# A fused attention and gate kernel: the first group's weights taken from the prepared tiles, the first loads on two DMA queues

## The reference

```
x   : 4 x 512 x 1024          xn = layernorm(x)
q, k, v = xn @ Wq.T, xn @ Wk.T, xn @ Wv.T     # 32 query heads, 8 key/value heads, 128 wide
q, k = rmsnorm(q) * q_norm_w, rmsnorm(k) * k_norm_w
scores = q k^T / sqrt(128) + slope[head] * (pos_k - pos_q), masked above the diagonal
s = softmax(scores) v  @ Wo.T
g = silu(xn @ W.T + bias + sum_n 2 * lora_weights[n] * (xn @ A_n.T) @ B_n.T)
out = x + s * g
```

## Time and profile before

| | before |
|---|---|
| median of 3 runs | 2731.64 us |
| profiled execution | 2726.47 us, span 2724.6 us |
| mean granted clock of TensorE | 0.985 |
| TensorE busy | 2591.6 us, 95% |
| VectorE, ACT, GpSimd busy | 1648.0, 1769.1, 1726.9 us |
| chain that ended last | TensorE 88%, VectorE 3%, ACT 2%, GpSimd 2%, DMA 2% |

### The profile page before, as it was taken

One profiled execution on the slowest core, in us unless ns is written; L12 is line 12 of the kernel. 1 busy time (PEld: TensorE's weight loads), 2 busy tenths in 40 slices (PEclk: granted clock), 3 DMA queues, 4 the chain that ended last, 5 costly groups with the idle time before them and its releaser, 6 DMA issues.

```text
span 2724.6 us, 39884 instructions
## 1 busy us (share of the span) xinstructions
PE 2591.6 (95%) x13840; PEld 2296.2 (84%) x13840; DVE 1648.0 (60%) x3520; ACT 1769.1 (65%) x4627; POOL 1726.9 (63%) x845
## 2 busy tenths in 40 slices
PE   2759999999999999999999999999999999999997
PEld 2648888888888888888888888888888888888886
DVE  4536655656667656566566665557566756555656
ACT  2246666666866766766776676666776667667763
POOL 2467787886667665656576666566565856656553
PEclk8879999999999999999999999999999999999999
DMA  7777778877345333433335433433334433433323
GB/s 234 261 263 262 251 249 274 266 257 247 118 149 166 117 122 111 142 113 103 119 94 175 149 109 115 141 110 111 109 107 142 165 122 99 122 117 109 116 69 128
DMA packets 183095, 424.48 MB, mean 156 GB/s; under 512 B 33520, under 2 KB 74608, under 8 KB 182000
## 3 DMA queue, kind: packets, MB, share of 16 engines
q1 hardware_dynamic: 182896, 421.93, 48.1%
HBM read 349.51 MB, written 89.13 MB: 161 GB/s over the span
## 4 chain that ended last, share of the span: by engine, by line
PE 88%; DVE 3%; ACT 2%; POOL 2%; DMA 2%; issue 1%; SPq 1%; POOLq 0%; DVEq 0%; ACTq 0%
PE proj L488 21%; PE proj L490 21%; PE proj L489 21%; PE tr L581 5%; PE sc L488 3%; PE sc L489 3%; PE sc L490 3%; PE ot L489 3%; PE tr L561 3%; PE ot L490 3%; PE ot L488 3%; POOL wl L926 1%; PE tr L554 1%; DVE acc L1166 0%; ACT prob L781 0%
## 5 line engine op out<-in xcount | busy, mean ns | idle before, releaser
L926 POOL TENSOR_TENSOR wl<-wl,wh 128x896 fp32r<-128x896 f32 x448 | 977.4, 2209 | 614.3 <-ACT wh L707 614.1
L488 PE MATMUL proj<-wh,xh 128*128 128x448 f32 x1792 | 674.0, 376 | 53.8 <-POOL wl L926 50.1
L489 PE MATMUL proj<-wl,xh 128*128 128x448 f32 x1792 | 661.2, 369 | 0.0
L490 PE MATMUL proj<-wh,xl 128*128 128x448 f32 x1792 | 661.1, 369 | 0.0
L937 POOL TENSOR_TENSOR wb_lo<-wb_lo,wb_hi 128x1024 fp32r<-128x1024 f32 x128 | 307.1, 2400 | 311.3 <-ACT wb_hi L717 311.3
L774 ACT ACTIVATE prob<-prob,negmax 128x128 f32<-128x128 f32 (+3 forms) x512 | 286.8, 565 | 250.3 <-DVE negmax L1144 250.3
L707 ACT ACTIVATE wh<-wl 128x896 fp32r<-128x896 f32 x448 | 406.3, 966 | 56.7 <-DMA wl<-wu 56.2
L488 PE MATMUL proj<-o_hi,wb_hi 128*128 128x512 f32 x1024 | 424.7, 415 | 9.2 <-issue 6.1
L1166 DVE TENSOR_TENSOR acc<-acc,proj 128x512 f32<-128x512 f32 x480 | 327.1, 683 | 156.6 <-PE proj L490 155.2
L753 ACT ACTIVATE pT_hi<-tr 128x512 fp32r<-128x512 f32 (+3 forms) x512 | 197.5, 440 | 334.8 <-PE tr L581 334.7
L488 PEld LDWEIGHTS proj<-wh,xh 128*128 128x128 f32 x1792 | 339.4, 189 | 86.7 <-issue 50.6
(11 more groups left out here) (121 smaller groups left out, 4339.3 us busy)
## 6 DMA issues: line engine op xcount, KB each, us to landing
wl<-wu SPq DMA_DIRECT2D x448, 448.0 KB, 3.9
wb_lo<-wo_in SPq DMA_DIRECT2D x128, 512.0 KB, 3.3
wu<-xtok SPq DMA_DIRECT2D x14, 1792.0 KB, 10.1
wo_in<-wo SPq DMA_DIRECT2D x32, 512.0 KB, 5.8
xtok<-wa SPq DMA_DIRECT2D x56, 256.0 KB, 4.4
wu<-xtok SPq DMA_DIRECT2D x14, 896.0 KB, 5.9
gate_dram<-z_buf SPq DMA_DIRECT2D x32, 256.0 KB, 5.1
xtok<-wa SPq DMA_DIRECT2D x56, 128.0 KB, 4.4
```

The lines of the kernel that those rows point to most:

```text
L488: pe.matmul(out, hi_l, hi_r, start=first, stop=False, skip_group_check=onto)
L489: pe.matmul(out, hi_l, lo_r, start=False, stop=False, skip_group_check=onto)
L490: return pe.matmul(out, lo_l, hi_r, start=False, stop=last, skip_group_check=onto)
L926: pool.tensor_tensor(w_slot(wl, w), w_slot(wl, w, True), w_slot(wh, w), ALU.subtract).then_inc(w_ready, 1)
```

## The change

The first group's tiles no longer go through memory before P1, P2, P6, P7, P4 and P5. ACT rounds them straight from the prepared tiles into `wh` (`split_first`), and GpSimd subtracts from the same place (`low_first`). The gate's 128 columns of group 0 are copied by ACT out of the merged rows as each is made (`gate_columns`), so the store to `weff` and the load from it are not in between. P3 is still loaded, and all of group 0 is still stored, since the later sequences read it.

The spaces are laid out anew. `prob`, `bias_sb`, `z_buf`, `e_buf` and `rel_sb` become parts of one tile `misc`, which also holds group 0's half 1 and before it the lora operands. The gate's rows of half 0 lie in `raw` (a piece can only be taken into `raw` once they are stored), those of half 1 in `xtok`. Group 1's half 0 is prepared in `acc`, its half 1 in `xtok`.

ACT's queue issues lora, identity, lora weights, constants and bias; SP begins with x. The bias has a semaphore of its own. VectorE does the statistics of x ahead of the lora factors. GpSimd makes its four sums of x between the low parts of P1, P2 and P6. VectorE makes the weight sums of group 0 between its low parts of x, and all eight sums of group 1 in step 0 of group 0 (before: half 0 on VectorE ahead of P3, half 1 on GpSimd ahead of group 1's P1). TensorE puts turns between the pieces of P1 and P2, and merges the gate's second half two by two in P6 and P7.

The order on SP, and the moved parts (other hunks rename places and counts in the same sense):

```diff
+            if half == 1:
+                return flat(xtok)[:, 512 * k:512 * k + 512]
+            return flat(raw)[:, 512 * k:512 * k + 512] if k < 7 else flat(acc)[:, 3584:4096]
+
+        lora_a_raw, lora_b_raw = misc[:, 0:TILE], misc[:, TILE:2 * TILE]
...
+                sp.wait_ge(prep_in[h], 192 * (g + 1) - 64)
+                if g == 0:
+                    sp.wait_ge(gate_cols, NK)
+                place = prep_place(g, h)
...
+            for t in range(NT):
                 sp.dma_start(xtok[:, t, :], x_first[:, t, :]).then_inc(x0_in[t], 16)
             load_gate_rows(0)
-            for dst, src in ((slope[:, 0:G], slopes), (qw_sb[:], qw), (kw_sb[:], kw)):
-                sp.dma_start(dst, src).then_inc(const_in, 16)
-            sp.dma_start(fb[:], ffn_b).then_inc(lw_in, 16)
             load_weights(0, 0)
             sp.wait_ge(lora_ready, 2)
             load_weights(0, 1)
-            store_gate_rows(0, range(NK))
-            sp.wait_ge(weff_out, 16 * NK)
-            for h in range(2):
-                load_gate_weights(0, h)
+            store_gate_rows(0)
             store_halves(0, 0)
             store_halves(0, 1)
-            load_product(0, P1)
-            load_product(0, P2)
+            sp.wait_ge(tr_done, TR["x", 0, 2 * NP - 1] + 1)
             load_gate_rows(1)
+            store_sums(0, 0)
             store_sums(0, 1)
-            store_sums(0, 0)
-            load_product(0, P6)
-            sp.wait_ge(tr_done, TR["x", 0, 2 * NP - 1] + 1)
+            store_gate_rows(1)
+            sp.wait_ge(weff_out[0], 16 * NK)
+            sp.wait_ge(prep_tst[0], 16)
+            sp.wait_ge(w_ready, 2 * P5 + 1)
             load_weights(1, 0)
             load_gate_weights(1, 0)
-            load_product(0, P7)
-            store_gate_rows(1, range(4))
-            load_product(0, P4)
-            store_halves(1, 0)
-            store_gate_rows(1, range(4, NK))
-            copy_b(0)
-            load_product(0, P5)
-            sp.wait_ge(weff_out, 32 * NK)
+            sp.wait_ge(prep_tst[1], 16)
+            sp.wait_ge(w_ready, 2 * P5 + 2)
             sp.dma_start(rel_sb[:], rel).then_inc(rel_in, 16)
             load_product(0, P3)
-            store_sums(1, 0)
-            sp.wait_ge(prep_tst[0], 16 * 2)
+            store_halves(1, 0)
+            copy_b(0)
+            sp.wait_ge(weff_out[1], 16 * NK)
             load_weights(1, 1)
             load_gate_weights(1, 1)
+            load_w(HW)
             store_halves(1, 1)
-            load_product(1, P1)
+            load_w(HW + 1)
             load_product(1, P2)
+            store_sums(1, 0)
```

TensorE, ACT, GpSimd and VectorE:

```diff
-            for f in range(4, 2 * NP):
+            for f in range(4, 7):
                 turn_x(("x", 0, f))
-            for p in range(NP):
+            for i, (p, t) in enumerate(((P1, 0), (P1, 1), (P2, 0), (P2, 1))):
+                piece(0, p, t)
+                if i < 3:
+                    turn_x(("x", 0, 7 + i))
+            for f in range(10, 2 * NP):
+                turn_x(("x", 0, f))
+            for i, (p, t) in enumerate(((P6, 0), (P6, 1), (P7, 0), (P7, 1))):
+                piece(0, p, t)
+                merge_gate(1, 2 * i)
+                merge_gate(1, 2 * i + 1)
+            for p in (P4, P5, P3):
                 for t in range(2):
                     piece(0, p, t)
-                    if 2 * p + t < NK:
-                        merge_gate(1, 2 * p + t)
...
+            def split_first(p):
+
+                a, c = {P1: (0, 0), P2: (1, 0), P6: (1, 1), P7: (0, 1), P4: (1, 0), P5: (0, 0)}[p]
+                for h in range(2):
+                    w = 2 * p + h
+                    if p in (P1, P2):
+                        act.wait_ge(prep_in[h], 128)
+                        act.wait_ge(gate_cols, NK)
+                    else:
+                        act.wait_ge(prep_t[h], 4 if p in (P4, P5) else 3)
+                        if h == 0:
+                            act.wait_ge(w_half, p - 1)
+                        else:
+                            act.wait_ge(u_done, u_count(0, p - 2, 1))
+                    act.activation(wh[:, w % 4], prep_tile(0, h, a, c), ACT.Copy).then_inc(w_hi_done, 1)
+
+            def gate_columns(k):
+
+                a, h, i = k // 4, k % 4 // 2, k % 2
+                act.wait_ge(weff_ready, k + 1)
+                at = 2 * a * 896 + i * HALF + 384
+                dst = prep_place(0, h)[:, at:at + 1024].rearrange("p (c n) -> p c n", c=2)[:, :, 0:64]
+                act.activation(dst, wt_slot(0, k)[:, 0:P].rearrange("p (c n) -> p c n", c=2), ACT.Copy
+                               ).then_inc(gate_cols, 1)
...
+            act.dma_start(lora_a_raw, lora_a).then_inc(lora_in[0], 16)
+            act.dma_start(lora_b_raw, lora_bt).then_inc(lora_in[1], 16)
+            act.dma_start(ident_sb[:], ident).then_inc(ident_in, 16)
+            for n in range(8):
+                act.dma_start(lw_sb[16 * n:16 * n + 16, :],
+                              lw[n:n + 1, :].to_broadcast([16, 1])).then_inc(lw_in, 16)
+            for dst, src in ((slope[:, 0:G], slopes), (qw_sb[:], qw), (kw_sb[:], kw)):
+                act.dma_start(dst, src).then_inc(const_in, 16)
+            act.dma_start(fb[:], ffn_b).then_inc(fb_in, 16)
             act.wait_ge(lora_in[0], 16)
             act.activation(lora_a_hi, lora_a_raw, ACT.Copy).then_inc(lora_hi, 1)
+            ln_rsqrt(0)
+            ln_scale(0, 0)
+            ln_scale(0, 1)
             act.wait_ge(lora_scaled, 1)
             act.activation(lora_b_hi, lora_b_raw, ACT.Copy).then_inc(lora_hi, 1)
-            ln_rsqrt(0)
-            for t in range(NT):
-                ln_scale(0, t)
-            for f in range(2 * NP):
+            ln_scale(0, 2)
+            ln_scale(0, 3)
+            for f in range(4):
                 x_hi(("x", 0, f))
-            act.wait_ge(qkw_ready, 1)
-            act.wait_ge(lw_in, 16 * 9)
-            split_product(0, P1)
-            split_product(0, P2)
-            act.wait_ge(prep_tst[1], 16)
-            for p in (P1, P2):
-                for t in range(2):
-                    take_piece(0, p, t)
-            split_product(0, P6)
+            for k in range(NK):
+                gate_columns(k)
+            split_first(P1)
+            for f in range(4, 7):
+                x_hi(("x", 0, f))
+            split_first(P2)
+            act.wait_ge(weff_out[0], 16 * NK)
+            for i, (p, t) in enumerate(((P1, 0), (P1, 1), (P2, 0), (P2, 1))):
+                take_piece(0, p, t)
+                if i < 3:
+                    x_hi(("x", 0, 7 + i))
+            for f in range(10, 2 * NP):
+                x_hi(("x", 0, f))
+            split_first(P6)
             for t in range(2):
                 square_rows(0, P2, t)
-            split_product(0, P7)
-            split_product(0, P4)
-            split_product(0, P5)
+            split_first(P7)
+            act.wait_ge(qkw_ready, 1)
+            act.wait_ge(fb_in, 16)
+            split_first(P4)
+            split_first(P5)
...
+            def low_first(p):
+                a, c = {P1: (0, 0), P2: (1, 0), P6: (1, 1), P7: (0, 1), P4: (1, 0), P5: (0, 0)}[p]
+                for h in range(2):
+                    w = 2 * p + h
+                    pool.wait_ge(w_hi_done, w + 1)
+                    pool.tensor_tensor(wl[:, w % 4], prep_tile(0, h, a, c), wh[:, w % 4], ALU.subtract
+                                       ).then_inc(w_ready, 1)
...
-            for p in (P7, P6, P5, P3):
-                x_sum(0, p)
-            low_product(0, P1)
-            low_product(0, P2)
-            for p in (P6, P7, P4, P5, P3):
-                low_product(0, p)
+            x_sum(0, P7)
+            low_first(P1)
+            x_sum(0, P6)
+            low_first(P2)
+            x_sum(0, P5)
+            x_sum(0, P3)
+            low_first(P6)
+            low_first(P7)
+            low_first(P4)
+            low_first(P5)
+            low_product(0, P3)
             pool.wait_ge(rel_in, 16)
             bias_of(0)
-            weight_sums(1, 1)
             low_product(1, P1)
             low_product(1, P2)
...
                 if p == P5:
                     dve.wait_ge(prep_bst[h], 32 * (g + 1))
+                    if g == 0:
+                        dve.wait_ge(w_ready, 2 * P1 + h + 1)
                     dve.tensor_tensor(b11, b12, b11, ALU.subtract).then_inc(prep_t[h], 1)
...
+            ln_stats(0, range(NT))
             dve.wait_ge(lora_in[1], 16)
-            dve.wait_ge(lw_in, 16 * 9)
+            dve.wait_ge(lw_in, 16 * 8)
             dve.tensor_scalar(lora_b_raw, lora_b_raw, lw_sb[:, 0:1], LORA_SCALE, ALU.mult, ALU.mult
                               ).then_inc(lora_scaled, 1)
-            ln_stats(0, range(NT))
+            ln_factors(0)
...
-            for f in range(4, 2 * NP):
+            for f in range(4, 7):
                 x_lo(("x", 0, f))
-            weight_sums(0, 1)
-            weight_sums(0, 0)
-            for k in range(4):
```

(21 more changed lines are left out.)

61 lines of the change are left out of this document (28 added, 33 removed).

## The result

| | before | after |
|---|---|---|
| median (four runs each) | 2731.59 us | 2696.5 us (2693.69 to 2701.62) |
| ratio after / before, 95% | | 0.9871 [0.9853, 0.989] |
| profiled execution, its span | 2726.47, 2724.6 us | 2694.11, 2692.3 us |
| mean granted clock | 0.985 | 0.989 |

Faster by 35.1 us in the medians (30 to 40 by the interval of the ratio) and by 32.3 in the spans; forecast were 41, and the time of 2696.5 lies inside the range of 2677 to 2709. The profiled execution of before was 5.1 us under its median and that after 2.4, so the spans show the smaller gain. The sign and the mechanism are right and most stations lie within 5 us; the gain in the sum is too large.

The account below looks back on a forecast made before the run. TensorE, busy 95%, bounds the kernel; only its 98.4 idle us in the first 240, a prologue chain of hand-overs, can be won. From gains of 38.5 and 42.7 it took 41: 2731.6 - 41 = 2690.6 us, range 2677 to 2709.

Parts of the forecast that it names:

- Start: Prologue's start: x issued first on SP, small DMAs on ACT's queue; x scaled at 14 to 16, 14 us earlier.
- At 0.5 they end at 9: ACT's 15 DMA issues at the start, taken at 0.5 us each, end at 9, under x's landing: cost 0.
- The bound of 1.3 us an issue: ACT's DMA issues at the start: at 1.3 us each they would end at 21 and cost 6 us.
- rival (c): Prologue's start: weff's store or ACT's issues hold the first products to 45 or later; gain 12 to 18, 2716; chance 0.06.
- Merge and P1: Group 0's merge and first product: 19 us through memory go; P1 starts at 35.2 against 66.83, 31.6 earlier.
- One op of each in 3.0 us: P2 to P6 of group 0: VectorE's weight sums and GpSimd's operations take turns, one of each in 3.0 us.
- Its price at the end, put at 6 us: P2 to P6 of group 0: 6 us less without the contention, 6 more with every sum at 3.0 us.
- P6 to P5: Group 0's P6, P7, P4, P5: TensorE sets the pace, 4.9 us a product, 1.4 per merge pair, 60 to 87.
- P3 and the first score: P3, still from memory: TensorE idles 4.8 us, P3 ends at 99 against 130.56, 31.5 earlier.
- SP's list: SP's queue from 78.6: 8 + 4 issues (3.97 for eight), then P3 and group 1; half 1's store issued at 100.1.
- rival (a): Hand-over to group 1 moves less: late half 1 transfers or VectorE sums all at 3 us; 25 to 30 remain, 2704; chance 0.25.
- Of 38.5 and 42.7 I take 41: Total gain: 41 us, chosen between 38.5 at group 2's loads and 42.7 at head 0's last attention product.

Follow-up runs that it names:

- e1: The changed kernel with the start of the kernel before (one queue on SP, old order, bias on the lora weights' semaphore, statistics behind lora factors): 2707.33 us.
- e5: The kernel before with only the changed start (ACT's queue, statistics first, a semaphore for the bias), weights still through memory: 2717.7 us.
- e2: The changed kernel with ACT's 15 DMAs back on SP's queue in the old order, bias semaphore and statistics first kept: 2699.35 us.
- e7: The changed kernel with VectorE's low parts of x (turns 8 to 13) put between group 0's weight sums: 2697.77 us.
- e12: The changed kernel with P3's two weight loads issued on SP ahead of group 1's weights: 2698.87 us.
- e6: The changed kernel with ACT's copy of head 0's fourth probabilities ahead of the split of group 1's P6: 2697.71 us.
- e8: The changed kernel with both ACT edits, e4's and e6's, together: 2690.03 us.
- e4: The changed kernel with ACT's splits of group 1's P1 and P2 moved behind head 0's exps and scaling: 2690.43 us.
- e10: e9 plus e6's edit, group 2's half 0 prepared in acc with loads issued earlier, and its GpSimd sums further ahead: 2687.69 us.
- e9: e4 with VectorE's sums of group 1's half 1 directly behind those of half 0, ahead of head 0's queries: 2688.22 us.

## Why the prediction was right, and where it was too high

| station | predicted | measured | gain predicted, measured |
|---|---|---|---|
| ACT's issues end | 9 | 8.96 | |
| x landed, scaled | 10.5, 14 to 16 | 12.4, 16.11 | 14, 13.4 |
| first sum of the merge | 25.6 | 25.52 | |
| P1 of group 0 | 35.2 | 35.02 | 31.6, 31.8 |
| last turn of x, P6 | 56.3, 60 | 55.68, 61.21 | 31, 29.95 |
| group 1's weights issued | 78.6 | 80.92 | |
| P3, first score | 93.1, 99 | 95.79, 103.12 | 31.5, 27.4 |
| half 1 stored | 100.1 | 104.65 | |
| first exp | 112.3 | 115.91 | 46.1, 42.5 |
| fourth probability turn | 133.2 | 136.55 | 44, 40.8 |
| last attention product | 140.3 | 148.63 | 42.7, 34.4 |
| group 2's loads | 135.6 | 140.43 | 38.5, 33.7 |
| end | | | 41, 32.3 (span) or 35.1 (median) |

*Start.* "At 0.5 they end at 9" was right: eight issues on ACT's queue took 4.71 us, 0.59 each. The bound of 1.3 us an issue, and rival (c), are out. x landed 2 us later than put, and the gain of its scaling was 0.6 us smaller. e1 and e5 show that what is won here comes through to the end; e2 that 2.8 us of it at x's scaling are the second queue and 11 the order and the semaphore. That fits the rule of the Trainium skill weighed in the prediction (DMA: Bandwidth & Descriptors, "Issuing engines are not separate DMA queues": only issue time is saved).

*Merge and P1.* Right within 0.2 us: the copies of the gate's columns took 0.31, only the last one counts, and the trip through memory is gone.

*Sums beside GpSimd.* "One op of each in 3.0 us" was right: 2.97 to 3.28. Its price at the end, put at 6 us, stays untested: e7 spread the sums out and gained no more than the scatter.

*P6 to P5.* The terms named, four products of 4.9 us and four pairs of merges of 1.4, make 25.2 us and not the 27 that were written down (60 to 87). Measured were some 28 (61.21 to 89.2), the first 2.8 of them at a granted clock of 0.50 after the wait ahead of P6. That the 27 came out near is thus in part luck.

*P3 and the first score.* Predicted a wait of 4.8; it was 5.56. The step mis-sized is the run of P3 behind it: put at 5 us by the earlier trace rows, it took 7.33, since TensorE came out of the wait at the lower of its two levels, 1.2 GHz (a granted clock of 0.50 until 100.78). The stretch of P3 of the two kernels, after first:

```profile
95.79:103.12 7.33, 7.33 (x24) 6.62 (x25) 1.84 (x3) 2.18 (x13) 3.47 (x2) 0.64 1.11 341
```

```profile
125.59:130.56 4.97, 4.97 (x27) 4.62 (x26) 4.94 (x7) 1.93 (x10) 0.77 (x1) 1.00 0.00 0
```

A granted clock of 0.64 against 1.00: products follow each other by 0.37 us until 100.8 and by 0.20 from there. Before, TensorE had been busy 7.37 of the 7.59 us ahead of P3; here 2.23 of 7.79. e12, without the wait, runs P3 at 1.00 in 5.19 us, and the end gains nothing.

*SP's list.* The eight issues were taken at 3.97, the row of a stretch with a DMA share of 0.72. In the new order the same eight took 6.42, and 9.63 at the start. The share of the DMA engines ahead of P3 (after, 88 us to P3's start):

```profile
88.00:95.79 7.79, 2.23 (x15) 1.88 (x14) 1.97 (x5) 2.64 (x4) 2.22 (x2) 0.90 1.06 367
```

Taken each over its own time, in the first 300 us of all kernels, eight such issues took 5.56 to 9.64 us in the 22 cases where the share was 1.00 or more, and 3.95 to 6.57 in the other 88; 3.97 was there at 0.60 as well as at 0.92 (e12). So a full DMA goes with longer issues, and a share a little below does not decide it. The kernel before had 5.95 for eight in its own start, at a share of 1.09: that row would have been the nearer one. With 2.3 us inherited at group 1's weights (80.92, put at 78.6), half 1's store is 4.5 us late, and rival (a)'s mechanism is there in part: the first exp gains 42.5 instead of 46.1.

*The sum.* Two things made it too large. "Of 38.5 and 42.7 I take 41, nearer to the row on PE's own chain" is a choice that no row backs, and it added 2.5 us to the smaller gain. And both gains were put too high: group 2's loads gained 33.7 instead of 38.5, the last attention product 34.4 instead of 42.7. Of the 4.8 us missing at the loads, 3.3 were there when the sums of half 1 were stored (132.22, put at 128.9), which goes back to SP's list above; the other 1.5 are mostly the landing of that store (6.8 us, put at 5.5).

The two stations moved alike in the changed kernel, so that it alone can't tell which of them counts. The experiments can. e6 and e8 move the attention product by 4.0 and 4.5 us and not the loads: nothing. e4 moves the loads by 5.9: 6 us in the median. e12 moves the first score 6.9 earlier and the loads 3.7 later: no gain. In all kernels but e10, score 7 comes 105.6 to 107.0 us behind the loads. What stands ahead of them is the chain store of halves, splits, exps, eight sums, store of sums, four loads of `wl`, and by e10 the bound is in that chain and in the loads of `wl`, not in group 2's loads that close it. The right size of the gain thus rests on SP's list, and the attention on which the forecast leaned is not what the time hangs on.

Three of the signs named were missed by little: x is scaled at 16.11 (14 to 16), the first score comes at 103.12 (97 to 102), the first exp at 115.91 (110 to 115). None of the signs of being wrong was there.

*Left open.* Whether the landing of the store, P6's second load or GpSimd's order is the bound behind `wl` was not separated: e10 moved the last two at once. Nor was it found why span minus loads varies between 2550.5 and 2557.6 from kernel to kernel; e10 has TensorE busy for all of 240 to 400 us (160.00), e9 156.57, and not the time that would go with it.

## What to carry to other kernels

Where groups hand buffers on in a ring, look in the trace for the first transfer of the steady part and for what releases its buffer. Here that station marked the time through prologues that differed by 40 us, while P3's wait of 5.6 us could be removed (e12) and attention brought 4.5 us forward (e8) without effect. But a mark is not yet a cause: move it apart from its neighbours, as e10 did in part, before you build on it, for what stands right ahead of it in the same queue may be what counts. When two stations give two gains, find out which one the time follows before you take a figure between them. And take the price of a DMA list from rows in which the DMA is as busy as it will be.

## What the runs showed of the hardware

- Eight issues of one kind on SP's queue took 3.95 to 6.57 us where the DMA share over them was below 1.00, and 5.56 to 9.64 where it was 1.00 or more (first 300 us of all kernels). In the changed kernel they took 6.42 at 1.02, 9.63 at 1.01 at the start, and 4.01 at 0.93 at 174.77. Eight issues on ACT's queue took 4.71.
- VectorE beside GpSimd pays for GpSimd's instruction, whatever its own size: 2.01 us for 128x8 elements in e4 (alone 0.16), 2.97 for 128x896 (alone 1.08). The Trainium skill has the lock (SBUF — State Buffer, "Who interferes with whom"); the trace agrees, and adds that small factors on the critical path are hit relatively hardest.
- After a wait of 5.56 us TensorE ran P3 in 7.33 us at a granted clock of 0.64, 2.4 us longer than the same product took at 1.00 in the kernel before (4.97) and 2.1 longer than in e12, which had no such wait (5.19).
